# Moving the set-up work of an adaLN, mLSTM and mixture-of-experts kernel to other places in its first two passes

## What is computed

```python
mod = (silu(c) @ wmod).reshape(8, 6, 1, -1)          # sa, ca, ga, sb, cb, gb
h = layernorm(x) * (1 + ca) + sa
x = x + ga * mlstm(h, norm_w, Wq, Wk, Wv, wi, wf, Wo, bo, Wout)
h = layernorm(x) * (1 + cb) + sb
x = x + gb * moe(h, Wr, br, W1, b1, W2, b2)

def moe(h):                                          # 8 experts, hidden 256, top 2
    top_w, top_i = top_k(h @ Wr + br, 2)
    gate = sum(one_hot(top_i) * softmax(top_w))      # token x expert
    y = einsum(relu(h @ W1[e] + b1[e]) @ W2[e] + b2[e])
    return einsum('te,eth->th', gate, y)
```

## Time and profile before

| | before |
|---|---|
| three runs, us | 358.61, 358.75, 359.09 |
| profiled execution, us | 354.73 |
| its span on the core, us | 353.0 |
| PE busy, share of the span | 91% |
| DVE busy | 79% |
| ACT busy | 45% |
| POOL busy | 48% |
| TensorE clock granted, mean | 0.984 |

### The profile page before, as it was taken

The page is one execution under the profiler, slowest core; times in us unless marked ns, Lnnn a source line. Parts: engine busy times, 40 slices in busy tenths (PEclk is TensorE's granted clock), DMA queues, the critical chain, the costliest instruction groups (busy, mean ns, idle before and its releaser), DMA issues.

```text
span 353.0 us, 4976 instructions
## 1 busy us (share of the span) xinstructions
PE 320.5 (91%) x1712; PEld 257.9 (73%) x1712; DVE 279.6 (79%) x799; ACT 158.6 (45%) x292; POOL 170.1 (48%) x177
## 2 busy tenths in 40 slices
PE   2999978799899998999899989998999989887995
PEld 2887865678587867887687858785888668665883
DVE  5576783699869996899699987999679967775774
ACT  1432423254454636545546554544545354244442
POOL 7610640158544772387417852485406821583340
PEclk9999996899999999999999999999999999999999
DMA  4850001500061005200160007000610053004301
GB/s 127 266 155 0 2 0 42 200 2 0 2 238 32 3 0 183 88 0 1 63 208 2 0 8 254 10 0 0 229 45 0 0 154 117 1 1 124 147 0 30
DMA packets 13710, 24.13 MB, mean 68 GB/s; under 512 B 1771, under 2 KB 8086, under 8 KB 12662
## 3 DMA queue, kind: packets, MB, share of 16 engines
q1 hardware_dynamic: 13458, 23.69, 20.7%
q10 hardware_dynamic: 164, 0.07, 0.1%
q0 software_dynamic: 64, 0.07, 0.1%
HBM read 21.59 MB, written 2.23 MB: 67 GB/s over the span
## 4 chain that ended last, share of the span: by engine, by line
PE 43%; DVE 37%; POOL 5%; DMA 4%; ACT 4%; issue 4%; SPq 1%; DVEq 0%; POOLq 0%
DVE hg L797 10%; PE bank L1000 5%; PE bank L1002 5%; PE bank L967 5%; PE bank L1001 5%; PE bank L1010 4%; PE bank L1009 4%; PE bank L1020 4%; DVE hg_lo L809 2%; PE bank L900 2%; DVE stats L560 2%; DVE m_row L773 2%; DMA gate_bc<-gates_d 2%; DVE zp L759 2%; DVE zo L748 2%
## 5 line engine op out<-in xcount | busy, mean ns | idle before, releaser
L446 POOL TENSOR_TENSOR hg_lo<-hg,hg_hi 128x512 fp32r<-128x512 f32 x69 | 88.1, 1286 | 81.2 <-ACT hg_hi L498 81.2
L797 DVE SCALAR_TENSOR_TENSOR hg<-bank,neg_b,gate_bc 128x512 f32<-128x512 f32 x128 | 94.6, 743 | 35.9 <-PE bank L1002 24.0
L498 ACT ACTIVATE hg_hi<-hg 128x512 fp32r<-128x512 f32 x128 | 79.7, 628 | 90.6 <-DVE hg L797 89.2
L1000 PE MATMUL bank<-h_hi,w_hi 128*128 128x512 f32 x128 | 58.4, 456 | 9.7 <-ACT gateT L542 9.7
L1010 PE MATMUL bank<-hg_hi,w_lo 128*128 128x512 f32 x128 | 51.1, 399 | 0.0
L1001 PE MATMUL bank<-h_hi,w_lo 128*128 128x512 f32 x128 | 50.9, 397 | 0.0
L1002 PE MATMUL bank<-h_lo,w_hi 128*128 128x512 f32 x128 | 50.8, 397 | 0.0
L1009 PE MATMUL bank<-hg_hi,w_hi 128*128 128x512 f32 x128 | 50.6, 395 | 0.0
L1020 PE MATMUL bank<-hg_lo,w_hi 128*128 128x512 f32 x128 | 50.5, 394 | 0.0
L415 POOL TENSOR_SCALAR var_eps<-mv 128x4 f32<-128x4 f32 x16 | 4.9, 305 | 80.4 <-DVE mv L566 80.4
L809 DVE TENSOR_TENSOR hg_lo<-hg,hg_hi 128x512 fp32r<-128x512 f32 x59 | 42.3, 718 | 0.5
(11 more groups left out here) (163 smaller groups left out, 552.4 us busy)
## 6 DMA issues: line engine op xcount, KB each, us to landing
gate_bc<-gates_d SPq DMA_DIRECT2D x8, 1024.0 KB, 7.1
gate_bc<-gates_d SPq DMA_DIRECT2D x16, 256.0 KB, 3.7
gate_bc<-gates_d SPq DMA_DIRECT2D x8, 512.0 KB, 4.9
out_dram<-x_all SPq DMA_DIRECT2D x8, 256.0 KB, 2.3
w_raw<-in_L_ffn_W_dram SPq DMA_DIRECT2D x1, 1024.0 KB, 8.6
x_all<-in_L_attn_x_dram SPq DMA_DIRECT2D x2, 256.0 KB, 3.8
wmod_sb<-in_L_wmod_dram SPq DMA_DIRECT2D x1, 384.0 KB, 4.4
gates_d<-gate_rows SPq DMA_DIRECT2D x8, 16.0 KB
```

Source lines behind the costliest of these rows:

```text
L446: g.tensor_tensor(hg_lo[k][:, :], hg[k][:, :], hg_hi[k][:, :].bitcast(fp32), ALU.subtract).then_inc(s_lo_pool, 1)
L498: a.activation(hg_hi[k][:, :], hg[k][:, :], ACT.Copy).then_inc(s_hghi, 1)
L797: v.scalar_tensor_tensor(hg[k][:, :], up_bank[n % 4][:, :], neg_b1[:, n:n + 1], gate_bc[own % 2][:, n // NU, :], ALU.max, ALU.mult).then_i ...
L1000: t_.matmul(dst, w_hi, hx, start=True, stop=False)
```

## The change

Work is written in other places; no computation is added or removed, except that PE has two turns less of `keep_busy` in the second pass and one group of it gives way to the bias products.

- PE: the 16 products b1 x W2 leave turn 12 of the first pass and stand at turn 3 of the second, in place of that turn's `keep_busy`, now in `y_bank`. `keep_busy` in the second pass ends with turn 12 instead of 14. The transpose of the gates moves from turn 14 to turn 13, ahead of the spread maximum. The wait for b2's low part moves from ahead of the second pass to the first down step, together with a wait for W2's low parts.
- DVE: `row_weights` goes from turn 17 to turn 12 of the first pass, two pieces of W1's low parts go later (turns 13 and 17), `b2_parts` goes from the end of the first pass to turn 17 of the second. In the second pass all four pieces of W2's low parts go to turn 16, ahead of the first `hg`; the last two multiplications of scores with weights go ahead of them; `m_row` goes behind the gates.
- POOL: in the second pass the order is rms at turn 6, norm(1) at 7, norm(0) at 11.

The diff, without its repeated signatures:

```diff
 # POOL body
-                    if t == 7 and end:
+                    if t == 7 and end and not opening:
                         norm(1, m1)
-                    if t == 8 and start:
+                    if t == (6 if opening else 8) and start:
                         pool.wait_ge(s_mse, m2 + 1)
...
-                    if t == 5 and ahead:
+                    if t == 7 and opening:
+                        norm(1, m1)
+                    if t == (11 if opening else 5) and ahead:
                         norm(0, b + 3)
 # DVE body
-                        if t == 12:
+                        if t == (13 if opening else 12):
                             dve.wait_ge(s_aT, m2 + 1)
...
-                        if t == 16:
+                        if t == 16 and not opening:
                             scores_times_weights(m2, 3)
                             scores_times_weights(m2, 2)
...
+                    if opening and t == N:
+                        scores_times_weights(m2, 3)
+                        scores_times_weights(m2, 2)
+                        for q in range(4):
+                            weights_lo(1, q)
                     if live(t):
...
-                    if first and t == 17:
+                    if first and t == 12:
                         row_weights()
...
-                    if first and t == 17:
+                    if opening and t == N + 1:
                         b2_parts()
-                    if first and t in (10, 11, 12, 13):
-                        weights_lo(0, t - 10)
-                    if end and not live(0) and t in (4, 8, 9, 10):
-                        weights_lo(1, (4, 8, 9, 10).index(t))
+                    if first and t in (10, 11, 13, 17):
+                        weights_lo(0, (10, 11, 13, 17).index(t))
 # PE body
-                    if first and t > LAG or opening and t < N - 1:
+                    if first and t > LAG or opening and LAG < t < N - 3:
                         keep_busy(2)
+                    if opening and t == LAG:
+                        b2_products()
...
-                            pe.wait_ge(s_wlo, 8)
+                            pe.wait_ge(s_wlo, 4)
                             pe.wait_ge(s_h2lo, 1)
...
+                        if b == 0 and n == 0:
+                            pe.wait_ge(s_wlo, 8)
+                            pe.wait_ge(s_b2l, 1)
                         pe.wait_ge(s_hghi, b * N + (n + 1))
...
-                    if t == N - 2 and end:
+                    if t == (N - 3 if opening else N - 2) and end:
                         pe.wait_ge(s_gates, b + 2)
...
-                    if first and t == 12:
-                        pe.wait_ge(s_b1, 1)
...
-            pe.wait_ge(s_b2l, 1)
             body(-1, True, True, True, lambda n: n >= N, opening=True)
```

More of the change, by code:

```diff
@@ L425, in norm, with body @@
                 g.tensor_tensor(xn[k][:, :, :], xn[k][:, :, :], bcast(rstd[k][:, :], D), ALU.mult).then_inc(s_xn[k], 1)
-            def body(b, end, start, ahead, live):
+            def body(b, end, start, ahead, live, opening=False):
                 m1, m2 = b + 1, b + 2
                 for t in range(LAG, N + LAG):
-                    if t == 7 and end:
+                    if t == 7 and end and not opening:
                         norm(1, m1)
-                    if t == 8 and start:
+                    if t == (6 if opening else 8) and start:
                         pool.wait_ge(s_mse, m2 + 1)
                         g.tensor_tensor(rms[:, :], ms_eps[:, :], minus_half[:, :], ALU.pow).then_inc(s_rms, 1)
-                    if t == 5 and ahead:
+                    if t == 7 and opening:
+                        norm(1, m1)
+                    if t == (11 if opening else 5) and ahead:
                         norm(0, b + 3)
@@ L455, in _ @@
             body(-2, False, True, True, lambda n: False)
-            body(-1, True, True, True, lambda n: n >= N)
+            body(-1, True, True, True, lambda n: n >= N, opening=True)
             for b in range(B - 3):
@@ L637, in b2_parts @@
                 for o in (0, LO):
-                    last = v.tensor_tensor(b2_raw[o:o + E, :], b2_raw[o:o + E, :], bank[2][o:o + E, 0:D], ALU.add)
+                    last = v.tensor_tensor(b2_raw[o:o + E, :], b2_raw[o:o + E, :], y_bank[o:o + E, 0:D], ALU.add)
                 last.then_inc(s_b2s, 1)
@@ L662, in scores_times_weights, with body @@
                 v.tensor_tensor(w, w, src, ALU.mult).then_inc(s_P, 1)
-            def body(b, end, start, ahead, live, first=False):
+            def body(b, end, start, ahead, live, first=False, opening=False):
                 m1, m2 = b + 1, b + 2
@@ L783, in after @@
                     if ahead and t == 4:
-                        if first:
-                            dve.wait_ge(s_xn[0], 1)
+                        dve.wait_ge(s_xn[0], b + 3)
                         norm_aggr(0, b + 3)
                 for t in range(LAG, N + LAG):
+                    if opening and t == N:
[3 more added lines that the diff above has]
+                            weights_lo(1, q)
                     if live(t):
@@ L974, in keep_busy, with b2_products @@
                     t_.matmul(bank[3][:, 0:P], ident[:, :], ones[:, :], start=True, stop=True)
+            def b2_products():
+                pe.wait_ge(s_b1, 1)
+                pe.wait_ge(s_w2, 16)
+                for n in range(N):
+                    last = t_.matmul(y_bank[0:LO + E, 0:D], b1_sel[:, n, :], w2_raw[:, n // NU, n % NU, :],
+                                     start=n == 0, stop=n == N - 1)
+                last.then_inc(s_b2w, 1)
             def body(b, end, start, ahead, live, first=False, opening=False):
                 for t in range(LAG, N + LAG):
-                    if first and t > LAG or opening and t < N - 1:
+                    if first and t > LAG or opening and LAG < t < N - 3:
                         keep_busy(2)
+                    if opening and t == LAG:
+                        b2_products()
                     if opening and t == 5:
```

## The result

The change makes the kernel slower. Over 20 runs of each the median is 359.98 us against 357.34 before. The ratio of the mean times is 1.0063 (95% interval 1.0033 to 1.0093); it leaves out two runs of the changed kernel that were over 1.5% above its fastest. A second series, ten runs of the changed kernel against 19 of the one before, gave 1.0083 (1.0043 to 1.0123). The forecast was 1.9 us, 0.53%; the two series measured 2.3 (0.0063 x 357.34) and 3.0 us.

What follows compares the result with a forecast made beforehand. It took one chain of waits through both early passes, with TensorE's clock at 1.2 GHz twice, as the bound; +2.75 to the copy and -0.9 behind it gave +1.85, so 358.75 + 1.9 = 360.6 us, range 358.0 to 362.4.

Steps and rivals of the forecast that it cites:

- First pass: First pass into second: `mb` 3.3 us and DVE 3.6 earlier, but the second pass's first transposes only 0.45 earlier.
- POOL: Second pass: rms at 43.3, ahead of the second norm, whose transposes on PE start at 48.0, 2.95 us later.
- Up to the copy: From the second norm's transposes to `gate_rows`: copy +2.75 us later in all, ends +0.75 and +3.75 depending on TensorE's clock.
- From the copy to the first full pass: From `gate_rows` to the transposes of `hh`: -0.9 us, ends -1.5 and +0.6; first down step 9.6 behind the copy.
- Sum: Whole kernel: +2.75 - 0.9 = +1.85 us, with the 0.45 and the 2.95 contained; total 360.6 us.
- third rival: Low clock from 48 to beyond 58 and through the first down and up steps: +4.35 us, 363.1; chance 0.08.
- the clock holds: PE's hole costs no clock in the second pass or first down step: -0.75 us, 358.0; chance 0.17.
- a draw: Clock falls only briefly and misses the spread maximum L952: about +0.2 us, 358.9; chance 0.17.
- The handed-back gain: Start of second pass: bias products behind L967 take back most of the first pass's 3.6 us; 0.45 remain.

Runs made afterwards that it cites:

- e4: Changed kernel with the 16 bias products two to a turn in turns 3 to 10 of the second pass, replacing keep_busy; 0.9968 of the kernel before.
- e2: Kernel before with only POOL's new second-pass order (rms, second norm, first norm of the other row) and its wait on DVE; 1.0101 of the kernel before.
- e1: Changed kernel with POOL's second norm ahead of rms again, the other row's first norm staying last; 0.9946 of the kernel before.
- e8: Changed kernel with POOL's order of before (first norm of the other row, second norm, rms); 0.9975 of the kernel before.
- e6: Changed kernel with ten more idle products on PE at turn 9 of the second pass, ahead of the second norm's transposes; 1.0073 of the kernel before.
- e11: Changed kernel with only the splitting of b2 on DVE moved to turn 4 of the second pass; 0.9965 of the kernel before.

## Why the prediction was right, and where its steps were off

The way that it told is the one that the traces show: the bias products hand the first pass's gain back, rms holds the second norm, PE idles ahead of it and the clock falls. The number is in part luck, as the sum below shows.

**First pass.** Forecast: `mb` 3.3 earlier, `den` 3.6 earlier, the second pass's transposes 0.45 earlier. Measured, less the 0.98 of the start: `mb` at 25.49 against 28.79 (3.3), `den` at 31.58 against 35.22 (3.6), the last product of the pass handing over to the bias products at 31.54 (31.5 forecast), the transposes at 35.64 against 36.30 (0.66). e4 confirms that the products held the rest.

**POOL.** Forecast: rms at 43.3, transposes at 48.0. Measured: 43.08 and 47.79. e2 shows that this order alone makes the kernel before slower, e1 that without it the change makes it faster.

**Up to the copy.** Forecast +2.75 with ends of 0.75 and 3.75; the trace has +3.62. Two steps were off. The clock was low from about 46 through the copy, which is the upper end, not the middle. And one edit was costed at nothing: "norm(0), moved last, has until the next pass". It has, but it runs beside the gates on DVE. From `lg` to the end of the gates I had 2.45; it took 3.34 in the changed kernel and 2.80 in e8 (the table's differences, and 0.19 for the last sum itself). The Trainium skill, SBUF — State Buffer, "Who interferes with whom", has the rule that a DVE instruction with two SBUF inputs contends with a GpSimd instruction that reads SBUF, and that the one issued second waits for the whole of the first; the 0.87 against 0.16 in e1 and e8 agrees. I had weighed it for the splitting of b2 alone.

**From the copy to the first full pass.** Forecast -0.9 with ends of -1.5 and +0.6; measured 15.13 against 14.38, **+0.75**: the mis-sized term, with the wrong sign. Its first half was right: the first down step came 9.45 behind the copy's start (9.6 forecast), with 3.2 of PE's wait for b2. Its second half was not: from there to hh it took 5.68 instead of about 4, all at 1.2 GHz. In e1 and e6, with about the same wait (3.2 and 3.0), it was 4.6. In e11, without the splitting in the way, the whole term was 10.4 instead of 15.1.

**Sum.** In this pair of traces +4.4, which is the third rival's 4.35, by the third rival's way. Behind hh another 1.65 came, which the prediction had at nothing: it took a shift there to shift the end by as much, and the late fall of the clock broke that. Over all runs it is +2.3 to +3.0 against +1.85 forecast. That the runs came so near is in part luck: in this pair of traces both terms were larger than forecast, and since one execution lies below its median and the other above, it is open what a typical pair would show. Luck is also in the total, 360.6 against the measured 359.98: the three runs that it started from, 358.75, were 1.4 above the median of the 20, 357.34, and the shift was too small. The 0.2% that the prediction says a measurement can tell is also too small: the intervals here reach 0.3% to 0.6% to either side. The rivals "the clock holds" and "a draw" did not come about.

**The handed-back gain.** The prediction took the 3.15 us (3.6 less 0.45) as given back for good ("What hid nothing before hides nothing now"). True for their new place, but there was a place that covers them: `keep_busy` issues instructions that take as long (0.64 us for four, against 0.63 in e4's row) in each of the turns behind.

## What to carry to other kernels

Before an instruction is moved ahead of another on the same engine, ask when each one's input is ready: rms waited for a value that came 2 us after the second norm's input, and so held a chain that needed 3.5 us more of the same engine. Set-up work that is moved off one chain should go where an engine is idle or runs filler, and the consumer named; here the bias products in the filler's place, b2 split ahead of the first hidden values with W2's low parts earlier, and POOL's old order together turned +0.6% into -2.4%. And a moved group must be costed for what runs beside it in its new place, on other engines too.

## What the runs showed that I had not expected

- A hole on PE that was filled moved the fall of the clock from about 46 to about 52.8, and the copy came only 0.7 us earlier (e6). In the second trace of before, full clock up to 63 instead of 51.7 gained 1.46 at the copy and nothing at hh.
- POOL's norm stretched single small DVE instructions of the gates from 0.16 to between 0.80 and 1.02 us (changed kernel, e1, e6).
- Of the parts of the change, POOL's order alone costs 1.0% (e2), while undoing either of two parts, this order (e1) or the place of b2's splitting (e11), brings the whole below the kernel before.
